# Order of the low-rank products and the transposes in the front part of a feed-forward stage

## The reference

```python
xf = layernorm(x).reshape(-1, 512)
gate_base = xf @ Wg.T ; up_base = xf @ Wu.T          # 512 -> 1408
base_out = silu(gate_base) * up_base @ Wd.T
probs = softmax(xf @ Wr.T)                            # router, 8 experts
topw, topi = top_k(probs, 2)
for e in range(8):                                    # low-rank experts, rank 16
    g_lora = xf @ Ag[e].T @ Bg[e].T * 2.0
    u_lora = xf @ Au[e].T @ Bu[e].T * 2.0
    h = silu(gate_base + g_lora) * (up_base + u_lora)
    acc += (h @ Ad[e].T @ Bd[e].T * 2.0) * weight_of_expert[e]
out = x + base_out + acc
```

## Time and profile before

| | us |
|---|---|
| median of 3 runs | 1084.57 (1083.83 to 1084.74) |
| the profiled execution | 1087.74 |
| its span (first to last instruction) | 1085.9 |
| stretch of the front part that the change touches | about 497 to 515 in the span |

### The profile page before, as it was taken

How to read it: one execution, slowest core, us unless ns; L and a number is a source line. 1 busy time by engine, 2 the same in 40 slices (tenths; PEclk the granted TensorE clock), 3 DMA queues, 4 the chain that set the end, 5 groups by cost and what they waited for, 6 DMA issues and landing times.

```text
span 1085.9 us, 13170 instructions
## 1 busy us (share of the span) xinstructions
PE 1046.4 (96%) x4867; PEld 845.7 (78%) x4867; DVE 600.7 (55%) x1041; ACT 448.7 (41%) x798; POOL 612.4 (56%) x452
## 2 busy tenths in 40 slices
PE   6999997899999999999999999999999999999998
PEld 4777775665689988876788888888888888888886
DVE  7999999848865644783622533325333253242224
ACT  5656443821575547554323323223322233322232
POOL 5878994210224562211266776667766667767662
PEclk9999998989999999999999999999999999999999
DMA  8512120000020020033222222533225332232211
GB/s 289 173 49 69 52 56 10 1 1 0 1 79 1 1 70 1 1 141 127 85 91 92 73 73 73 170 139 122 73 73 170 114 129 90 73 112 92 82 65 39
DMA packets 24543, 85.48 MB, mean 79 GB/s; under 512 B 3152, under 2 KB 4832, under 8 KB 23712
## 3 DMA queue, kind: packets, MB, share of 16 engines
q1 hardware_dynamic: 22432, 81.24, 22.0%
q10 hardware_dynamic: 2048, 3.41, 0.9%
HBM read 74.86 MB, written 9.78 MB: 78 GB/s over the span
## 4 chain that ended last, share of the span: by engine, by line
PE 63%; DVE 1%; POOL 1%; issue 1%; ACT 0%; POOLq 0%
PE banks L318 20%; PE banks L320 20%; PE banks L319 20%; PE banks L313 1%; PE banks L1427 1%; POOL wgl L635 0%; DVE stat L1690 0%; PE banks L1436 0%; POOL gul L661 0%; DVE xres L2071 0%; POOL xtr L618 0%; ACT xn L773 0%; DVE xf L1958 0%; PE banks L1492 0%; DVE hf L2082 0%
## 5 line engine op out<-in xcount | busy, mean ns | idle before, releaser
L2082 DVE TENSOR_TENSOR hf<-banks,silu 128x512 f32<-128x512 f32 x132 | 91.3, 692 | 323.9 <-PE banks L320 322.6
L661 POOL TENSOR_TENSOR gul<-wst,guh 128x1280 fp32r<-128x1280 f32 x44 | 129.9, 2952 | 141.7 <-DVE guh L1965 135.8
L671 POOL TENSOR_TENSOR hl<-hf,hh 128x512 fp32r<-128x512 f32 x129 | 178.0, 1409 | 8.9 <-ACT hh L1049 8.9
L1049 ACT ACTIVATE hh<-hf 128x512 fp32r<-128x512 f32 x132 | 83.6, 633 | 190.3 <-DVE hf L2082 190.3
L1085 PE MATMUL banks<-kv,strip 128*128 128x288 f32 x640 | 157.3, 406 | 1.2 <-DVE pr L1665 1.2
L1047 ACT ACTIVATE silu<-banks 128x512 f32<-128x512 f32 x132 | 78.9, 598 | 167.5 <-PE banks L320 167.4
L1085 PEld LDWEIGHTS banks<-kv,strip 128*128 128x128 f32 x640 | 120.7, 190 | 34.0 <-issue 1.6
L318 PE MATMUL banks<-xf,guh 128*128 128x512 f32 x352 | 137.2, 390 | 0.9 <-POOL gul L661 0.9
L319 PE MATMUL banks<-xf,guh 128*128 128x512 f32 x352 | 136.9, 389 | 0.0
L320 PE MATMUL banks<-xf,gul 128*128 128x512 f32 x352 | 136.9, 389 | 0.0
L595 POOL TENSOR_TENSOR rstd<-vare,mhalf 128x2 f32<-128x2 f32 x32 | 25.5, 796 | 165.7 <-DVE vare L1699 165.7
(11 more groups left out here) (289 smaller groups left out, 2238.9 us busy)
## 6 DMA issues: line engine op xcount, KB each, us to landing
wst<-in_chunk_w SPq DMA_DIRECT2D x44, 960.0 KB, 4.7
strip<-toep SPq DMA_DIRECT2D x29, 256.0 KB, 3.0
xf_s<-xf SPq DMA_DIRECT2D x2, 2048.0 KB, 6.8
out<-xres SPq DMA_DIRECT2D x16, 256.0 KB, 2.1
xf<-xf_s SPq DMA_DIRECT2D x8, 512.0 KB, 5.8
mk<-hot_s SPq DMA_DIRECT2D x14, 256.0 KB
xres<-in_x ACTq DMA_DIRECT2D x4, 512.0 KB, 7.1
xres<-in_x SPq DMA_DIRECT2D x2, 1024.0 KB, 5.7
```

The lines of the kernel that those rows point to most:

```text
L661: pool.tensor_tensor(gul[:, u, :], wst[:, u, 0:GU_W], f(guh[:, u, :]), ALU.subtract).then_inc(gul_ready, 1)
L671: pool.tensor_tensor(hl[:, u, s, :], hf[:, s, :], f(hh[:, u, s, :]), ALU.subtract)\
L1049: act.activation(hh[:, u, s, :], hf[:, s, :], ACT.Copy).then_inc(hh_ready, 1)
L2082: dve.tensor_tensor(hf[:, s, :], banks[:, 7, :], silu[:, s % 2, :], ALU.mult).then_inc(mul_done, 1)
```

## The change

On TensorE `lora_a(1, 0)` moves from behind `logits_f(2)` to a place ahead of `turn_f(12)`. `lora_a(1, 1)` is cut in two: its first two blocks now stand behind `logits_f(2)`, and its last two where the whole call stood. On ScalarE `keep_a(1, 0)` moves ahead of `high_f(12)`. No instruction is added or taken out.

```diff
@@ ScalarE
             high_f(10)
             high_f(11)
             apply(TILES + 15)
+            keep_a(1, 0)
             high_f(12)
             high_f(13)
             logits_copied(2)
-            keep_a(1, 0)
             high_f(14)
             high_f(15)
             keep_a(1, 1)
@@ TensorE
             turn_f(10)
             turn_f(11)
             by_token_f(1)
+            lora_a(1, 0)
             turn_f(12)
             turn_f(13)
             logits_f(2)
-            lora_a(1, 0)
+            lora_a(1, 1, 0, 2)
             turn_f(14)
             turn_f(15)
             by_token_f(2)
-            lora_a(1, 1)
+            lora_a(1, 1, 2)
             logits_f(3)
             lora_a(2, 0, 0, 1)
             by_token_f(3)
```

## The result

| | before | after |
|---|---|---|
| median, 20 executions each | 1084.65 us (1082.69 to 1088.60) | 1082.39 us (1080.47 to 1085.38) |
| profiled execution, its span | 1087.74, 1085.9 | 1082.37, 1080.5 |

The ratio is 0.9975, 95% interval 0.9966 to 0.9983: 2.26 us between the medians, and anything from 1.8 to 3.7 us by the interval. Two executions of one kernel differ by more than that, so the traces are read piece by piece.

The account below looks back on a forecast made before the run. TensorE, busy 1046.4 of 1085.9 us, was taken to bound the kernel. Terms of -1.60, -0.36, -1.52, -0.04 and +0.20 sum to -3.32; 3.3 off the median 1084.57 gives 1081.3 us, range 1080.3 to 1083.7.

Parts of the forecast that it names:

- the masks' transposes: Sign in the profile after: on TensorE, behind `by_token_f(3)`, these transposes would stand at 520.4 us.
- The layout: TensorE's new order, priced piece by piece: from `by_token_f(1)` at 497.33 to `by_token_f(3)` at 511.44, where it was 514.75.
- The idle time: TensorE's wait for VectorE between `by_token_f(1)` and `turn_f(12)` would go: 1.60 us gained.
- the slow logits: `logits_f(2)`, at half clock after the pause, would fall from 3.37 to 1.85 us: 1.52 us gained.
- The slower pair of transposes: Transposes of tiles 12 and 13, after the pause, would fall from 1.23 to 0.87 us: 0.36 us gained.
- the restart: One more restart of TensorE, after the small products of `by_token_f(1)`, would cost 0.20 us.
- the 0.04 beside it: The slower start of `lora_a(1, 0)` would go, 2.84 to 2.80 us: 0.04 us gained.
- three pauses with a fall of the clock behind them: TensorE idle times of 2.11, 1.70 and 1.53 us, each followed by a stretch at 0.50 of full clock.
- The waits: Waits on ScalarE's and VectorE's results would stay covered and cost zero; `logits_f(3)` would keep 1.0 us of cover.
- The loop: From 528 to 1083 us, TensorE busy at full clock; its end would move as much as its start.
- The first rival: The slow clock near `logits_f(2)` was not in the timed runs: gain only 1.76 us, 1082.8 us; chance 0.30.

Follow-up runs that it names:

- the filler: The kernel before with six matmuls of unused result added ahead of `turn_f(12)`, no useful work moved: ratio 0.9993, median 1084.15 us.
- products only: The kernel after with only TensorE's part of the change, `keep_a(1, 0)` staying behind `logits_copied(2)` on ScalarE: ratio 0.9981, median 1083.02 us.
- three in the hole: The kernel before with only the first three products of `lora_a(1, 0)` moved ahead of `turn_f(12)`: ratio 0.9983, median 1083.13 us.

## Why the prediction was right

The median is 1082.39, in the range of 1080.3 to 1083.7 and 1.1 above the 1081.3 I named. The ratio's interval lies wholly below 1, on the side that I had forecast, and holds 3.3 us at its far side. With the 2.15 us that arose ahead of the change added back, `by_token_f(3)` starts at 511.51, the masks' transposes at 520.43 and the span is 1082.65, each within 0.15 us of what I had.

- **The layout** was right in every piece: 14.11 us predicted, 14.11 in the chain, and 14.15 or 14.16 in each of the five traces in which the hole is filled with the moved products. The idle time (1.60) went as priced, and the slow logits nearly so: 1.48 in the timeline (3.41 less 1.93), where I had 1.52.
- **One term had the wrong cause and size.** The slower pair of transposes was not an effect of the pause: it was the wait of `turn_f(13)`, as the filler showed, and 0.19 us instead of 0.36. It goes with the change all the same, since the products give VectorE the time. That the sum came within 0.1 us of 3.24 is in part luck: the restart that I had added at 0.20 and the 0.04 beside it are +0.02 together in the timeline, where all products of `lora_a(1, ...)` take 5.78 us before and 5.80 after, and the two errors cancel.
- **One place was overlooked.** I counted three pauses with a fall of the clock behind them. There is a fourth, the longest: TensorE waits 6.95 us until 188.19, and the clock is at 0.50 from 183.6 to 193.8. It lies ahead of the change and enters no term.
- **The waits** stayed covered, and the tightest, `logits_f(3)`, had 1.06 us where I had 1.0. Leaving ScalarE's move out changed nothing in the trace.
- **The loop** carried the gain to the end: 571.2 us from `by_token_f(3)` on in both.
- **The first rival** (no slow logits in the timed runs) was the right worry with the wrong size. I gave it 0.30 for all of the timed executions. Six profiles of six had the slow logits.

What of 3.3 is missing in the medians? I pooled 69 executions of the kernel before from two sets of experiments (the single one at 1084.14 us among them; one of 1089.94 us at a mean clock of 0.942 is left out) and all 32 of the kernel after: the means are 1085.21 and 1082.52, 2.69 us apart, with a standard error of 0.34 from the two scatters. Two standard errors to each side, 2.0 to 3.4 us, take in 3.3 at the edge. So scatter may be all of it. Two causes could each make up the rest, and the record does not choose between them.

The first is the share of executions with slow logits. Equal mean clocks don't give it away. At 0.992 the kernels lie at 1084.0 and 1082.3 (medians of 33 and 9), at 0.997 at 1082.26 and 1080.57 (5 and 6), 1.7 us apart each time; but equal clocks mean equal slow time in all, and the one trace at 0.992 of the kernel before had the slow logits. The group at 0.997 says more: its slow time is 2 x 0.003 x 1081 = 6.5 us in all, about what the pause near 184 takes by itself at its shortest in any trace here (6.8). So these 5 executions of the 69 should have had fast logits. With 1.76 + 1.56 times the share equal to 2.69, the share is 0.6 (0.2 to 1 within two standard errors). Six of six has a chance of 0.05 at 0.6, and the profiled executions have a lower mean clock (0.988) than the 69 (0.991), so they may not be a fair draw.

The second lies ahead of the change, where the kernels are alike. From the start behind the 1.70 us of pause to `by_token_f(1)` it is 215.63 us in the first trace of the kernel before, with a slow stretch near 283, and 214.15 in the trace at 1084.14, without one: 1.5 us. Of the six traces of the kernel before three have that stretch, of the seven of all other kernels seven. If the timed executions were like that, half of those of the kernel before would be 1.5 us shorter by something that the change does not touch, 0.75 us in the mean, and 3.24 would come down to 2.5 with slow logits in every one. Thirteen traces are too few to say so.

That the share is below one is thus argued from five executions; its size stays open. Not shown is a trace of the kernel before with fast logits.

**The clock, from run to run.** That the number of slow matmuls differs between runs of the same kernel (the Trainium skill, TensorE: Matmul & The Clock Gate, Part 1) agrees with the traces: the slow stretch behind the pause near 233 lasted 3.4 us in some and 10.2 in others, and in two of them (products only, three in the hole) it was missing. That transposes count less as work (the same page of the Trainium skill, Part 4) was not seen to matter: transposes and small products side by side ran at 1.00 in all five traces that have them after the moved products.

## What to carry to other kernels

A pause of TensorE can cost more than its own length, by the slow stretch that follows it: here 1.6 us of pause brought 3.4 us at half clock and with them 1.5 us more. So the first products put into such a hole can be worth the most; three of twelve gave 2.24 of 3.24 us in the trace. Look for work whose operands were ready two steps earlier, lay out the new order from start-to-start times, and judge a change of 0.2% by the length of its own stretch in traces of like pattern, not by medians of a dozen executions.

## What the hardware showed

- The same kernel against itself gave 1.0018 (1.0005 to 1.0031) in one set of runs. But for the one at 0.942, its undisturbed executions run from 1082.1 to 1089.1 us, with the mean clock from 0.997 down to 0.986. Much of the scatter goes with the time that TensorE spends at 1.2 GHz, but not all in proportion: eleven executions at 0.993 took 1085.5 to 1087.2 us, and 33 at 0.992 only 1083.4 to 1084.8.
- What a slow stretch costs depends on the work in it. The 3.4 us near 283, where TensorE has no wait, cost 1.5 us. The 10.2 us behind the pause of 2.11 us cost 2.1: from the start behind that pause to the one behind the 1.70 us it is 48.13 us with them and 45.99 without them (three in the hole), and without them TensorE waits for VectorE in between.
- The same pause can bring a slow stretch in one execution and none in the next. The one of 1.7 us ahead of 281.70 brought one in three of the six profiles of the kernel before, and in all seven traces of the other kernels. The one of 2.1 us ahead of 233.57 brought none in two traces (products only, three in the hole). The one of 1.53 us that the change fills brought one in six of six, and one of 0.64 us in its place none in the one trace that has it.
